# First image's head of a two-layer analog-conv + attention kernel: weight sums moved between engines, rows handed over by pair, own slots for the second image's chain

## The reference

```python
v   = round(clip(gn(x) * input_factor, -1, 1) * 127) / 127 * 0.6    # dac
fv  = pad(v) + 0.1 * pad(v)**3                                      # cubic; spatially transposed, 3x3 patches
g   = g_pos - g_neg                                                 # three planes [o, c, 3, 3]
out_i = einsum(patches(fv), g[i])                                   # i = 0, 1, 2: three 3x3 convolutions
y   = sum of clip(round(out_i*0.01*256)/256, -16, 16) with weights 4, 2, 1 (+1)
x1  = x + y * output_factor + bias

z   = gn(x1); q, k, v = Wq z, Wk z, Wv z                            # second layer, 1x1
o   = q * (exp(B) (exp(k) v)) / (exp(B) exp(k))
x2  = x1 + Wm o
```

## Time and profile before

| | before |
|---|---|
| median of 3 runs (lowest to highest) | 1509.46 us (1508.66 to 1511.33) |
| the profiled execution | 1513.01 us |
| its span, first to last instruction | 1511.2 us |
| PE busy | 1431.6 us (95%) |
| DVE busy | 1357.5 us (90%) |
| ACT busy | 1192.5 us (79%) |
| POOL busy | 578.4 us (38%) |
| granted TensorE clock, mean of the span | 0.981 |

### The profile page before, as it was taken

The page is one execution under the profiler, slowest core; times in us unless marked ns, Lnnn a source line. Parts: engine busy times, 40 slices in busy tenths (PEclk is TensorE's granted clock), DMA queues, the critical chain, the costliest instruction groups (busy, mean ns, idle before and its releaser), DMA issues.

```text
span 1511.2 us, 24709 instructions
## 1 busy us (share of the span) xinstructions
PE 1431.6 (95%) x8560; PEld 658.8 (44%) x8560; DVE 1357.5 (90%) x2029; ACT 1192.5 (79%) x1562; POOL 578.4 (38%) x689
## 2 busy tenths in 40 slices
PE   2799999999999999999999999999999999999975
PEld 2444444444444444444444444444444444444432
DVE  6879899999989999998999999999999989999756
ACT  5547788897978888897888889788888888886553
POOL 3211435243353534344353433435343443534322
PEclk9799999999999999999999999999999999999988
DMA  5011002323123222312322231232223123212232
GB/s 210 1 56 34 24 16 55 98 57 111 31 55 112 57 85 57 112 38 55 105 57 84 57 113 41 55 104 57 85 57 112 42 57 98 56 29 57 57 84 84
DMA packets 29186, 103.96 MB, mean 69 GB/s; under 512 B 4032, under 2 KB 4224, under 8 KB 29056
## 3 DMA queue, kind: packets, MB, share of 16 engines
q1 hardware_dynamic: 20416, 70.86, 12.6%
q0 software_dynamic: 8640, 31.46, 11.0%
HBM read 37.29 MB, written 33.55 MB: 47 GB/s over the span
## 4 chain that ended last, share of the span: by engine, by line
PE 48%; DVE 28%; issue 11%; ACT 7%; POOL 4%; DMA 1%; DVEq 0%; SPq 0%; POOLq 0%; ACTq 0%
PE A L506 8%; PE A L508 8%; PE A L507 8%; PE B L506 5%; PE B L508 5%; PE B L507 5%; DVE f L1115 3%; PE L L588 3%; PE L L619 3%; DVE duo L1138 2%; ACT q L751 2%; PE B L641 2%; ACT T L771 2%; POOL T L1549 2%; DVE t L1150 1%
## 5 line engine op out<-in xcount | busy, mean ns | idle before, releaser
L506 PE MATMUL A<-T,WH 128*128 128x504 f16 (+1 forms) x1152 | 439.1, 381 | 0.0
L507 PE MATMUL A<-T,WH 128*128 128x504 f16 (+1 forms) x1152 | 438.1, 380 | 0.0
L508 PE MATMUL A<-T,WL 128*128 128x504 f16 (+1 forms) x1152 | 438.0, 380 | 0.0
L1549 POOL TENSOR_TENSOR T<-t,T 128x512 f16<-128x512 f32 x189 | 257.6, 1390 | 285.1 <-ACT T L771 285.1
L1523 POOL TENSOR_TENSOR zl<-z,zh 128x512 f16<-128x512 f32 x120 | 154.5, 1304 | 394.3 <-ACT zh L882 394.3
L814 ACT ACTIVATE junk<-xr,shift 128x1024 f16<-128x1024 f32 x244 | 280.1, 1148 | 5.4
L506 PE MATMUL B<-T,WH 128*128 128x504 f16 (+1 forms) x576 | 222.1, 386 | 20.0 <-DVE T L1164 11.5
L507 PE MATMUL B<-T,WH 128*128 128x504 f16 (+1 forms) x576 | 221.9, 385 | 0.0
L508 PE MATMUL B<-T,WL 128*128 128x504 f16 (+1 forms) x576 | 221.7, 385 | 0.0
L506 PEld LDWEIGHTS A<-T,WH 128*128 128x128 f16 x1152 | 115.6, 100 | 166.2 <-issue 48.7
L508 PEld LDWEIGHTS A<-T,WL 128*128 128x128 f16 x1152 | 112.9, 98 | 136.7 <-issue 0.8
(11 more groups left out here) (192 smaller groups left out, 2568.4 us busy)
## 6 DMA issues: line engine op xcount, KB each, us to landing
xr<-in_x_dram SPq DMA_DIRECT2D x64, 512.0 KB, 5.6
out_dram<-xr SPq DMA_DIRECT2D x64, 512.0 KB, 2.7
xr<-shared POOLq DMA_DIRECT2D x60, 512.0 KB, 4.6
xr<-in_L_conv_g_pos_dram SPq DMA_DIRECT2D x3, 576.0 KB, 10.0
xr<-in_L_conv_g_neg_dram SPq DMA_DIRECT2D x3, 576.0 KB, 11.1
xr<-in_L_conv_Wm_dram SPq DMA_DIRECT2D x2, 32.0 KB, 9.2
xr<-in_L_conv_Wq_dram SPq DMA_DIRECT2D x1, 32.0 KB, 11.8
xr<-in_L_conv_Wk_dram SPq DMA_DIRECT2D x1, 32.0 KB, 11.6
```

What stands on the lines that cost most here:

```text
L506: nc.tensor.matmul(to, wh, th, start=fresh and y == 1, stop=False, skip_group_check=True)
L507: nc.tensor.matmul(to, wh, tl, start=False, stop=False, skip_group_check=True)
L508: done = nc.tensor.matmul(to, wl, th, start=False, stop=y == 2, skip_group_check=True)
L1549: last = nc.gpsimd.tensor_tensor(low, t32[:, pair, :, :, :].rearrange("p t e w -> p (t e w)"), high, ALU.subtract)
```

## The change

What it does, in the order of the program:

- SP no longer issues the three small transfers; ACT issues them as its first instructions, before its table load.
- The difference of plane 0 is made on DVE (in the head, behind `spread_head`), that of plane 2 on DVE in slot 0 of phase 0; that of plane 1 stays on POOL, behind `scale_x`.
- Plane 0's four sums are gone. DVE makes only `left` and `far`; PE adds and subtracts in PSUM (`turn_first`: 10 float32 products instead of 6 for a turn, with the identity, minus, half and minus-half identity, which POOL makes at the start).
- Planes 1 and 2: ACT scales five pieces each (`scaled_parts`), POOL makes two edge sums and four sums each (`edge_sums`, `weight_sums`). DVE makes none of them.
- `head_rows_low` on DVE is gone; POOL makes the low rows of group 1.
- In all images `transform` makes pair 2 first, then pair 1, then pair 0, and reports each (`t_ready`), `rows_high` takes them one by one, `rows_low` reports each (`tl_ready`), and PE waits for pair 2 ahead of j = 2, for pair 1 ahead of j = 4, for pair 0 ahead of j = 0 of a half's first plane.
- Turns 3 to 8 stand in slots 1, 2, 2, 6, 8, 9; turn 4 goes to the free tile A1 instead of L.
- Image 0's group 2 is transformed in slot 0 of phase 0. Phase 0 has a slot table of its own (`FIRST`) for the second image's chain.

```diff
-LEVEL = (17, 19, 20, 24)
-TRANSFORM = (26, 29, 3, 11)
+EACH = {"X_STATS": (0, 2, 4, 6), ..., "LEVEL": (17, 19, 20, 24), ..., "TRANSFORM": (26, 29, 3, 11), ...}
+FIRST = {"X_STATS": (2, 4, 5, 7), "X_SPREAD": 8, "X_GROUP": 10, "X_MOMENTS": 9,
+         "LEVEL": (11, 12, 14, 17), ...
+         "TRANSFORM": (21, 27, 0, 6), "HIGH": (25, 30, 1, 9), "LOW": (25, 30, 2, 9)}
+TURN = {1: (3,), 2: (4, 5), 6: (6,), 8: (7,), 9: (8,)}
...
+PAIRS = (2, 1, 0)
...
 def turn_pair(n):
+    return (A[0], A[1], last_pair, last_pair, A[1], last_pair)[min(n, 5)]
...
+            def turn_first(y):
+                if y == 0:
+                    pe.wait_ge(const_step, 9)
+                    pe.wait_ge(first_parts, 2)
+                    pe.wait_ge(first_sums, 2)
+                d, bank = tap_weights(0), turned(y)
+                half, left, far = (parts[:, k, y, :] for k in (0, 2, 3))
+                sums_of = (((d[:, 0, y, :], ident),), ((left, ident), (half, ident)), ((left, ident), (half, minus_eye)),
+                           ((far, ident), (half, minus_half)), ((far, ident), (half, half_eye)), ((d[:, 2, y, :], eye4),))
...
+            def turn_weights(n):
+                i, y = divmod(n, 3)
                 if y == 0:
-                    pe.wait_ge(sums_made, i + 1)
+                    pe.wait_ge(sums_made, i)
-                if n >= 3:
-                    pe.wait_ge(w_done, n)
+                if n != 4:
+                    pe.wait_ge(w_done, 4 if n == 5 else n)
...
+            def rows_read(p, h, pair):
+                at = nth(p, NP * NG, NP * (2 * h + 1) + PAIRS.index(pair))
+                pe.wait_ge(th_ready, at)
+                pe.wait_ge(tl_ready, at)
...
             def rows_high(image, parity, g):
-                act.wait_ge(t_ready, nth(image, NG, g))
...
-                for pair in range(3):
+                for k, pair in enumerate(PAIRS):
+                    act.wait_ge(t_ready, nth(image, NP * NG, NP * g + k))
...
+            def scaled_parts(i, which):
+                d = tap_weights(i)
+                act.wait_ge(w_diff[i], 1)
+                for k in which:
+                    x, c = ((2, -CSCALE / 6), (0, -CSCALE / 6), (0, CSCALE / 24), (1, -CSCALE / 6), (1, -CSCALE / 12))[k]
+                    nc.scalar.activation(pieces_of(i)[k], d[:, x], ACT.Identity, scale=c).then_inc(scaled, 1)
...
             level(0, 0, 1)
             cubic(0, 0)
             cubic(0, 1)
+            high_weights(0)
             level(0, 0, 2)
-            cubic(0, 2)
-            high_weights(0)
-            rows_high(0, 0, 0)
-            rows_high(0, 0, 1)
+            high_weights(1)
+            level(0, 0, 3)
+            rows_high(0, 0, 0)
+            cubic(0, 2)
+            cubic(0, 3)
+            high_weights(2)
+            scaled_parts(1, (0, 1, 2))
+            rows_high(0, 0, 1)
+            scaled_parts(1, (3, 4))
+            scaled_parts(2, range(5))
...
+            weight_difference(0)
             group_moments(0, 0)
-            weight_sums(0)
+            first_weight_sums()
+            quantise(0, 0)
             quantise(0, 1)
             cubic_f(0, 0)
             cubic_f(0, 1)
...
+            transform(0, 0, ())
             quantise(0, 2)
-            transform(0, 0, ())
+            quantise(0, 3)
+            low_weights(0)
             cubic_f(0, 2)
...
             transform(0, 1, ())
-            head_rows_low(1)
-            weight_sums(1)
...
+            def edge_sums(i):
+                right, left, far = pieces_of(i)[0:3]
+                pool.wait_ge(scaled, 5 * (i - 1) + 3)
+                nc.gpsimd.tensor_tensor(left, left, right, ALU.add).then_inc(parts_made, 1)
+                nc.gpsimd.tensor_tensor(far, far, right, ALU.subtract).then_inc(parts_made, 1)
+            def weight_sums(i):
+                left, far, half, quarter = pieces_of(i)[1:5]
+                pool.wait_ge(scaled, 5 * i)
+                pool.wait_ge(parts_made, 2 * i)
+                nc.gpsimd.tensor_tensor(U[:, i, 0], left, half, ALU.add)
...
-            weight_difference(0)
             scale_x(0)
             weight_difference(1)
             rows_low(0, 0, 0)
-            pool.wait_ge(sums_made, 2)
-            weight_difference(2)
+            edge_sums(1)
+            rows_low(0, 0, 1)
+            weight_sums(1)
+            edge_sums(2)
+            weight_sums(2)
```

263 lines of the change are left out of this document (133 added, 130 removed).

## The result

| | before | after |
|---|---|---|
| median of four runs (lowest to highest), us | 1510.39 (1508.66 to 1511.49) | 1502.00 (1501.34 to 1502.58) |
| profiled execution, us (span) | 1513.01 (1511.2) | 1501.34 (1499.6) |
| first product of image 0 | 41.09 | 40.56 |
| first product of image 1 | 137.34 | 128.82 |
| last image, PE behind DVE L1304 / L1347 | 1453.79 | 1445.09 |

A forecast was written before the change was run, and what follows sets the result against it. PE was taken to bound the kernel from phase 2 on. Terms 4.3 + 6.2 + 1.5 + 2.3 + 1.7 - 1.8 gave 14.2 us, 14.5 by the points; 1509.46 - 14.5 = 1495.0 us, range 1487.5 to 1502.5.

The forecast's parts named there:

- The debt: Time PE loses up to image 1's first product; later phases, being PE-bound, neither add to it nor pay it back.
- the two gaps with their half clock: PE's idle gaps before 63.2 and 137.34 us; the half-clock stretches behind them were priced at 2.8 and 1.7 us.
- The new waits: PE waits forecast at turn 3 (3.8 us, POOL's sums), step 1 (0.7) and step 3's j = 1 (1.8, ACT).
- first product at 36.8: Image 0's first PE product at 36.8 us, 4.3 us earlier than before; bounds 35 and 39.
- POOL's plane difference 1 then holds off the first `quantise` until about 18.4: In the head, before the first product: the first `quantise` waits for POOL until 18.4 us, against 20.84 before.
- nothing [...] to one microsecond: Price of the three small transfers going first on another queue; their 1.4 us of issue end before the first load lands.
- Turns: DVE and POOL instructions exclude each other in strict turn; 512 elements on POOL hold DVE off 0.9 us.
- The wait of 3.8 us: Phase 0, turn 3: PE waits 3.8 us for POOL's first four sums, made at 46.3 us.
- rival 2: Later sums, step 2 near 79, ACT waits of 3 us at two steps; gain 8 us, 1501.5 us; chance 0.22.
- 1.8 for ACT: Between step 2 and image 1, at step 3's j = 1: PE waits 1.8 us for ACT's rounding.
- I take 0: Steady images: no change in time per image, bounds -0.3 to +0.2 us per image.
- The rival from the Trainium skill: By its engine rule, GpSimd being about 2x slower, POOL's sums would come later and the change lose; no chance given.

The follow-up runs named there:

- f2: The changed kernel with POOL's two edge sums of plane 1 behind its low rows of group 1 instead of ahead; 1503.32 us, 0.9955 of the kernel before.
- f4: The changed kernel with small transfers on SP, turns 3 to 5 a slot later, plane 2's difference behind `transform(0, 2)` and its follow-up work later; 1507.42 us, 0.9981.
- g1: The changed kernel with `transform(0, 2)` on DVE behind `WL` 3 and its casts on ACT behind `WH` 5; 1500.27 us, 0.9924 of the kernel before.
- e3: The changed kernel with PE waiting for all three pairs of a half ahead of j = 2, as before the change; 1500.81 us, 0.9928.
- h1: The changed kernel with the hardware loop over images 6 to 13 written out; 1498.95 us, 0.9918 of the kernel before.
- h3: The kernel before the change with the same hardware loop written out; 1507.52 us, 0.9973 of the kernel before.
- e4: The changed kernel with the second image's chain in phase 0 in the slots that all images have; 1501.67 us, 0.9931 of the kernel before.
- e1: The changed kernel with the three small transfers back on SP, behind plane 0's weights; 1500.46 us, 0.9925 of the kernel before.
- h4: The changed kernel with small transfers on SP, `transform(0, 2)` behind `WL` 3, its casts behind `WH` 5, and the loop written out; 1498.22 us, 0.9911.

## Why the prediction was right and wrong

**Right: what bounds the kernel, and where the gain comes from.** The debt is made before image 1, steady images keep PE's pace (87.24 busy of 87.70), and the two gaps with their half clock went. The new waits stand where they were forecast. That the time fell inside the range at all is helped by its width: two errors beyond my bounds, the start and the loop, both went against me.

**Wrong: "first product at 36.8".** It came at 40.56, 3.8 us late and beyond my upper bound of 39; image 1 is 4.3 us short. The step that failed first is "POOL's plane difference 1 then holds off the first `quantise` until about 18.4". I let that difference start at once behind the scale, at 15.4, and it started at 17.62 and ended at 20.25. `transform(0, 0)` followed at 24.13 instead of 22.1: 2.0 of the 3.8 us. Two things stand behind it. The small transfers made the image's last piece land 1.5 us later on average, and the moments and the scale with it; but with the transfers on SP again the first product gains only 0.6 us (1.0 with both forms of the head mixed). So my price for them of "nothing [...] to one microsecond" at the first product holds, though not my reason, the 1.4 us of issue: the loads are what they delay. The rest would have been lost without them: with the transfers on SP the difference started at 16.8 to 17.5, in five of these seven traces behind its own load. The earlier trace rows showed that load, at 16.91 behind a wait for DMA, and I left it out.

**Wrong in size: DVE beside POOL.** Turns were the right picture (f2: 0.42 against 1.12 and 1.21 us), but I priced them too low at each place. In the head I had 9.9 us from `transform(0, 0)` to `transform(0, 1)`. It took 11.2, of which 0.85 is the long form of the head: bad luck of this execution, since 10.35 is what ten traces have. DVE's `q` pair took 2.67 us there beside POOL's low rows, where a pair alone takes 0.75. From the first product to turn 3 it took 10.2 instead of 9.5: a 384-element sum on POOL takes 1.00 us alone, not the 0.83 I wrote (the line that I named gives 0.86), and the last two low rows took 4.20 beside DVE's difference instead of 3.08 (f4). From turn 3 to step 1 it took 12.2 instead of 11.2, since `transform(0, 2)`, more than doubled in length by the sums, stands ahead of `WL` 3; g1 got 1.2 us back by moving it. These are 3 of the missing 6 us. Behind step 1 about 1.1 came back: step 2 started at 80.3.

**Wrong: what the hand-over by pair is worth.** I put 4.3 us of the gain down to an earlier start. e3 starts 4.7 us later and loses nothing: at turn 3 PE waits for POOL anyway. The wait of 3.8 us that I forecast there myself should have told me that the start doesn't count. What counts up to there is when POOL's sums are made. My rival 2, the later sums and 1501.5, is what happened up to step 2, which it had near 79. Its long waits for ACT did not come: PE waited 0.5 us for ACT in step 3 and 0.3 for DVE in step 5, where I had 1.8 for ACT.

**Wrong: behind image 1 "I take 0".** Per image that held. The bounds I gave were for things that repeat, and what cost 1.5 us happens once: the loop's back-jump, a term that the sum doesn't have. DVE's stall is 3.9 instead of 2.7 us there and reaches PE. h1 and h3 show it: 2.8 against 1.3 us. Image 1 short by 4.3 and the jump by 1.5 are the 5.8 us between a lead of 14.5 and one of 8.7.

**The rival from the Trainium skill** ("GPSIMD Engine Reference", Engine selection: two-input elementwise work on VectorE) would have had the change lose, and as a whole it gained: image 1 starts 8.5 us earlier. How much of that is the sums' place is not shown, since no run puts only them back on DVE. What the rule has right is that the sums on POOL are what turn 3 now waits for.

**Open:** which part of the change brings the 8.5 us at image 1. PE's wait by pair (e3), the second image's own slots (e4) and the transfers (e1) bring nothing or harm, so it lies in what is left: the sums and differences on other engines, the low rows of group 1 on POOL, the earlier turns, and the ten products of plane 0's turns. No run takes one of these away. Open too is why DVE's stall at the jump is longer in every version of the changed kernel (3.8 to 4.0 us in all thirteen traces with the loop) than in both of the kernel before (2.7, 2.8). Nine instructions more ahead of the loop changed it by 0.1 only; a loop body of another length wasn't tried. Last, the edits of h4 show less in the medians than in PE's marks. Part of that can be the stretch behind the last mark, which comes up to 2.9 us longer at the lower clocks; how often each clock is granted there in executions without a trace, no run tells.

## What to carry to other kernels

When an engine's work is moved to one with which it takes turns on SBUF, price each pair of instructions that will run side by side, not only those at the place you look at, and put what is not urgent behind what is. A new wait cancels whatever was won ahead of it, so an earlier start is worth nothing until the next wait on the same engine has been passed. When an instruction is put earlier in a queue, look up when its own load lands. And look at what happens once: the order in which the first transfers go out (0.6 to 1.0 us) and the back-jump of a hardware loop (1.5) together took 2 to 2.5 us of the 14.5 forecast here. And when two single traces are compared, check first what differs between executions of one kernel: here the form of the head alone moves the marks by 0.85 us, and the clock at the end the span by up to 2.9.

## What the runs showed of the hardware

- Three transfers of 128 rows of 4 bytes, issued on ACT's queue at 0.8 to 2.2 us, held up four loads of 512 KB on SP's queue: the last landed at 10.38 us on average (eight traces) instead of 8.87 (seven) with them behind on the same queue.
- DVE's and POOL's instructions on SBUF stretched each other when side by side, as if in turn: 0.42 us became 1.1 to 1.2 for DVE (256 elements), while 384 elements on POOL went from 1.00 to 1.17 or 1.44, once to 1.98. DVE's `WL`, which reads PSUM, took 0.94 to 0.96 with and without POOL beside it.
- At the back-jump of the hardware loop DVE stood idle 2.7 to 4.0 us; with the loop's eight images written out there is no such stall, and both kernels were faster (by 1.3 and 2.8 us in PE's marks). PE's own idleness put down to nobody was 0.47 us there (910.78).
- TensorE's granted clock differs between executions of the same work: in the 10 us behind the last mark it was 1.00, 0.83 or 0.66, and the stretch to the end took 54.5, 55.2 to 56.5 and 57.4 us.
